# The shift of both LayerNorms moves from VectorE to GpSimd, in a cross-attention and expert kernel

## The reference

```
h  = layernorm(x)                        # over the 1024 positions, eps 1e-5
q, k, v = Wq h + bq, Wk ctx + bk, Wv ctx + bv      # 128x128 weights over the channels
att = softmax over a window of 16 keys around each position, 8 heads of 16 channels
x  = x + Wo att(q, k, v) + bo
g  = layernorm(x)                        # second LayerNorm
w  = top-2 of softmax(g @ gate_w.T) over 8 experts, renormalised
x  = x + sum_e w[:, e] * (g @ A_e.T @ B_e.T)       # rank 64 per expert
layernorm(x) = (x - mean) / sqrt(var + eps)
```

## Time and profile before

| what | value |
|---|---|
| median of 3 runs | 1264.25 us (1264.19 to 1271.45) |
| profiled execution, its own time | 1263.59 us |
| span of its trace | 1261.8 us |
| mean granted TensorE clock | 0.916 |
| one step of the batch loop | 35 to 40 us |

### The profile page before, as it was taken

The page is one execution under the profiler, slowest core; times in us unless marked ns, Lnnn a source line. Parts: engine busy times, 40 slices in busy tenths (PEclk is TensorE's granted clock), DMA queues, the critical chain, the costliest instruction groups (busy, mean ns, idle before and its releaser), DMA issues.

```text
span 1261.8 us, 55007 instructions
## 1 busy us (share of the span) xinstructions
PE 1074.9 (85%) x24452; PEld 909.8 (72%) x24452; DVE 898.5 (71%) x1922; ACT 574.4 (46%) x809; POOL 416.9 (33%) x306
## 2 busy tenths in 40 slices
PE   4658898988989888998988989888988888989986
PEld 2547786776778677776776878677876777877875
DVE  3567777776768767777776778777677776778873
ACT  4545535444545444444444444444454444455431
POOL 3563323333323233233333223233233333323220
PEclk8778998889989889988989989989988989989999
DMA  4422233123232123232123232123231232332210
GB/s 169 121 70 53 70 87 80 47 67 87 70 86 72 51 70 86 71 86 66 57 70 87 70 87 66 59 67 87 71 86 42 64 86 71 87 86 69 55 36 34
DMA packets 157313, 92.87 MB, mean 74 GB/s; under 512 B 139680, under 2 KB 139808, under 8 KB 156704
## 3 DMA queue, kind: packets, MB, share of 16 engines
q1 hardware_dynamic: 157088, 89.25, 25.4%
HBM read 55.16 MB, written 16.78 MB: 57 GB/s over the span
## 4 chain that ended last, share of the span: by engine, by line
issue 43%; POOL 20%; PE 16%; DVE 13%; ACT 4%; DMA 2%; SPq 1%; POOLq 0%; DVEq 0%
PE bank_a L310 8%; POOL prob L911 8%; POOL ctx_split L917 5%; PE bank_c L310 3%; POOL x_split L943 3%; PE bank_b L360 3%; POOL attn_split L934 2%; DVE row_max L744 2%; DVE row_sum L758 1%; PE bank_b L339 1%; DMA raw<-x 1%; ACT k_sb L575 1%; DVE prob L750 1%; SPq L246 1%; DVE stats L673 1%
## 5 line engine op out<-in xcount | busy, mean ns | idle before, releaser
L911 POOL TENSOR_TENSOR prob<-prob,row_inv 128x512 f32<-128x512 f32 x128 | 134.4, 1050 | 427.8 <-DVE row_inv L762 426.1
L360 PEld LDWEIGHTS bank_b<-prob_t,v_diag 64*64 64x64 f32 x4608 | 214.3, 148 | 49.2 <-issue 26.2
L360 PE MATMUL bank_b<-prob_t,v_diag 64*64 64x96 f32 (+2 forms) x4608 | 228.8, 257 | 15.4 <-DMA v_diag<-v_t 14.4
L310 PE MATMUL bank_a<-down_split,mid_split 128*128 128x264 f32 (+1 forms) x1536 | 215.9, 289 | 8.5 <-issue 6.8
L310 PEld LDWEIGHTS bank_a<-down_split,mid_split 128*128 128x128 f32 x1536 | 194.8, 189 | 16.5 <-issue 8.6
L769 DVE STREAM_TRANSPOSE prob_t<-prob 128x768 f32<-128x768 f32 x128 | 124.9, 976 | 111.8 <-POOL prob L911 110.6
L310 PE MATMUL bank_a<-up_split,ht_split 128*128 128x512 f32 x768 | 194.3, 402 | 3.5 <-DVE ht_split L859 3.5
L558 ACT ACTIVATE prob<-prob 128x512 f32<-128x512 f32 x128 | 80.8, 631 | 248.5 <-DVE prob L750 248.3
L339 PEld LDWEIGHTS bank_b<-k_sb,q_diag 32*32 32x32 f32 x16384 | 153.4, 104 | 39.5 <-issue 33.3
L339 PE MATMUL bank_b<-k_sb,q_diag 32*32 32x32 f32 x16384 | 169.1, 194 | 9.3 <-issue 6.5
L310 PEld LDWEIGHTS bank_a<-up_split,ht_split 128*128 128x128 f32 x768 | 141.0, 190 | 34.1 <-ACT ht_split L634 3.4
(11 more groups left out here) (76 smaller groups left out, 1360.6 us busy)
## 6 DMA issues: line engine op xcount, KB each, us to landing
v_diag<-v_t SPq DMA_DIRECT2D x128, 132.0 KB
raw<-x SPq DMA_DIRECT2D x32, 512.0 KB, 4.1
resid_pair<-x SPq DMA_DIRECT2D x32, 512.0 KB, 4.4
out<-resid_pair SPq DMA_DIRECT2D x32, 512.0 KB, 2.6
raw<-ctx SPq DMA_DIRECT2D x31, 512.0 KB, 3.6
prob_t<-up_w SPq DMA_DIRECT2D x1, 1024.0 KB, 6.3
resid_pair<-up_w SPq DMA_DIRECT2D x1, 1024.0 KB, 5.7
v_diag<-down_w SPq DMA_DIRECT2D x1, 1024.0 KB, 7.6
```

Source lines behind the costliest of these rows:

```text
L310: return nc.tensor.matmul(dst, st[:, s, st_cols], mv[:, m, mv_cols], start=start and n == 0, stop=stop and n == 2)
L360: last = nc.tensor.matmul(bank_b[2 + m % 2][rows, lo * PW:hi * PW], value_blocks(b)[rows, n, :], prob_t[rows, at:at + (hi - lo) * KT], sta ...
L911: nc.gpsimd.tensor_tensor(weights_of(m), weights_of(m), row_inv[:, cols].unsqueeze(2).broadcast_to([P, CT, KT]), ALU.mult).then_inc(prob_d ...
```

## The change

VectorE no longer computes the shift. Instead it computes the negated mean right behind `var_eps` (a `tensor_scalar` of one element), and GpSimd multiplies it with `rstd` right behind its power, after a wait on its own power. ScalarE waits for the new semaphores `shift1` and `shift2`. `var_eps` gets a second column per norm. No order of any engine is changed otherwise.

```
-        var_eps = sb("var_eps", [P, 2])
+        var_eps = sb("var_eps", [P, 2, 2])
...
+        shift1, shift2 = sem("shift1"), sem("shift2")
...
                 if later:
-                    act.wait_ge(ln1_step, later.count(6, 6))
+                    act.wait_ge(shift1, later.count(1, 1))
...
                 if prev:
-                    act.wait_ge(ln2_step, prev.count(6, 6))
+                    act.wait_ge(shift2, prev.count(1, 1))
...
-                nc.vector.tensor_scalar(var_eps[:, which:which + 1], moments[:, which, 1:2], EPS, None,
+                nc.vector.tensor_scalar(var_eps[:, which, 0:1], moments[:, which, 1:2], EPS, None,
                                         ALU.add).then_inc(semaphore, 1)
-
-            def layernorm_shift(which, semaphore, batch):
-
-                nc.vector.scalar_tensor_tensor(shift[:, which:which + 1], moments[:, which, 0:1], -1.0,
-                                               rstd[:, which:which + 1], ALU.mult,
-                                               ALU.mult).then_inc(semaphore, 1)
+                nc.vector.tensor_scalar(var_eps[:, which, 1:2], moments[:, which, 0:1], -1.0, None,
+                                        ALU.mult).then_inc(semaphore, 1)
...
                 if later:
                     first_norm()
-                    first_shift()
...
-                if prev and not cur:
-                    second_shift()
...
                     join_heads(cur, 1)
-                    if prev:
-                        second_shift()
...
+            def rows_norm(which, step_done, ready, b):
+
+                pool.wait_ge(step_done, b.count(6, 6))
+                nc.gpsimd.tensor_tensor(rstd[:, which:which + 1], var_eps[:, which, 0:1], consts[:, 2:3],
+                                        ALU.pow).then_inc(ready[0], 1)
+                pool.wait_ge(ready[0], b.count(1, 1))
+                nc.gpsimd.tensor_tensor(shift[:, which:which + 1], var_eps[:, which, 1:2],
+                                        rstd[:, which:which + 1], ALU.mult).then_inc(ready[1], 1)
...
                 if later:
-                    pool.wait_ge(ln1_step, later.count(6, 5))
-                    nc.gpsimd.tensor_tensor(rstd[:, 0:1], var_eps[:, 0:1], consts[:, 2:3],
-                                            ALU.pow).then_inc(rstd1, 1)
+                    rows_norm(0, ln1_step, (rstd1, shift1), later)
...
                     if prev:
-                        pool.wait_ge(ln2_step, prev.count(6, 5))
-                        nc.gpsimd.tensor_tensor(rstd[:, 1:2], var_eps[:, 1:2], consts[:, 2:3],
-                                                ALU.pow).then_inc(rstd2, 1)
+                        rows_norm(1, ln2_step, (rstd2, shift2), prev)
```

More of the change, by code:

```diff
@@ L802, in second_norm @@
                     layernorm_stats(1, resid[prev.parity], ln2_step, prev)
-                def second_shift():
-                    dve.wait_ge(rstd2, prev.count(1, 1))
-                    layernorm_shift(1, ln2_step, prev)
                 def first_norm():
@@ L812, in first_norm @@
                     layernorm_stats(0, raw, ln1_step, later)
-                def first_shift():
-                    dve.wait_ge(rstd1, later.count(1, 1))
-                    layernorm_shift(0, ln1_step, later)
                 if cur:
```

## The result

The changed kernel took 1287.47 us (median of 4 runs, 1285.57 to 1296.89), the kernel before 1266.51 us beside it (4 runs): ratio 1.0177, 95% interval 1.0129 to 1.0225. So the change costs some 21 us. The profiled execution of the changed kernel is its slowest one, 1296.89 us with a span of 1295.1, so its span is some 9 us longer than that of the median run; the reading goes by single steps.

The account below looks back on a forecast made before the run. It took a slackless loop through `h_sb` to bound the kernel, TensorE being nearly the bound. With `h_sb` 0.70 us later in 28 steps, +19.6 us on 1263.59 gives 1283 us; range 1250 to 1292.

Parts of the forecast that it names:

- The loop and its leverage: Batch loop: no slack, so a shift of `h_sb` by D moves each step by D while TensorE still waits; 28 steps.
- GpSimd's chain: GpSimd, first norm: own wait 0.06 us, multiplication 0.20; shift ready at 606.45, `attn_split` starts at 606.42 and its delay is hidden.
- L709 passes with a margin of 0.02: Gate chain on VectorE: L709 at 606.23 falls between the power's end and the multiplication at 606.25, so is not held.
- the first rival: Gate chain: L709 or the cast meets the multiplication and is held to `attn_split`'s end; 1250 us, or 1260; chance 0.17.
- its mixtures: Some steps as forecast, others with L709 too late; half and half 1266 us, other mixtures 1255 to 1278; chance 0.12.
- L716 is held to the end of `attn_split`: Gate chain on VectorE: two-input L716, due at 607.04, is held to 608.81, giving back the 2.32 us and 0.33 more.
- `x_split` is ready early and holds the rest: GpSimd: `x_split` starts at 608.96 instead of 611.88, runs 2.35 us to 611.31 and holds the gate chain's last steps.
- Which step it holds: Under `x_split`: L719's second half is held, `h_sb` 0.70 us later; if only L723 is held, 0.44.
- by turns: Rival: steps fall either way between forecast and L709 arriving too late; +3 us at half and half, 1266; chance 0.12.
- The mis-sized term: Per step, `h_sb` starts 0.70 us later (bounds 0.39 to 1.22), in 28 steps: +19.6 us.
- No price for the clock: TensorE: no further clock loss priced, as it runs at 0.50 behind these waits already; a longer wait might stretch that.
- The second norm at nothing: Second norm: xn starts some 0.2 us later, covered by ScalarE's 1.07 us idle; costs nothing, else 0.2 us a step.

Follow-up runs that it names:

- e1: Changed kernel, with GpSimd waiting for the gate chain's end before `x_split`; 1198.85 us, ratio 0.9446 against the kernel before.
- e5: Kernel before, plus GpSimd's added wait and a multiplication into an unused tile, the shift staying on VectorE; 1246.66 us, ratio 0.985.
- e4: Kernel before, with VectorE's shift as a `tensor_scalar` taking `rstd` as scalar operand instead of a second tensor input; 1233.54 us, ratio 0.9732.
- e6: Changed kernel, with `attn_split` ahead of the power and first-norm shift in GpSimd's order, no further wait; 1132.1 us, ratio 0.8907.

## Why the prediction was right

It said 1283 us, 28 x 0.70 = 19.6 us above the profiled execution; measured were 21 us between the medians, and 1287.47. By its own steps:

- *The loop and its leverage* (each step moves by what `h_sb` moves): 28 x (6.42 - 5.62) = 22 us against 21 between the medians. In the other direction it understates: e1, e5 and e4 gained 68, 22 and 34 us where 28 steps give 39, 14 and 22. Between the profiled executions, path and fall of TensorE's busy time add up well there (58, 22 and 28 us for spans shorter by 61, 22 and 28). So that the path alone gives the change's 21 us is in part luck, as the clock below shows.
- *GpSimd's chain*: wait and multiplication about as costed. The wait took 0.08 us for 0.06 and the shift 0.19 for 0.20, and `attn_split` started 1.06 us behind `var_eps` where the prediction had 1.08.
- *L709 passes with a margin of 0.02*: as L706 it started 0.03 to 0.04 us ahead of the multiplication in all 28 steps. Its longest in the whole trace is 0.153 us, so the first rival came in none of the steps. The range of 1250 to 1266 that I kept for it and for its mixtures was not needed. The cast did not fall between power and multiplication, by the prediction's own figures either: it starts 0.04 us before the power ends (606.15 against 606.19; measured 580.52 against 580.56). It was not held, and the further powers show that a power holds nothing, so "held while GpSimd runs a `TENSOR_TENSOR`" was too wide.
- *L716 is held to the end of `attn_split`*: 583.21 against 583.19, with a start 1.69 behind `var_eps`, predicted 1.70. It is L713 in the changed kernel.
- *`x_split` is ready early and holds the rest*: started 3.62 behind `var_eps`, predicted 3.62.
- *Which step it holds*: a pick, as taken by the nearest row, the cast, and not the sum, which kept 0.17 us. It is the second pick, as worked out, in 17 steps; in 11 it is the first, which the prediction had starting 0.12 us ahead of `x_split` and passing. This went by turns, not L709. The rule of the Trainium skill ("VectorE: DVE Perf Modes", section "Mode 2×_2P") fits the trace: eight elements from one input are held (2.66 us for the two picks), one element is not; that they ran in that mode no run here shows. The other rule of the Trainium skill ("SBUF — State Buffer", section "Who interferes with whom"), that whoever issues first has the port, fits e5 and both kernels with further powers, but not by the starts in the trace when they are close: a pick that started 0.09 us before `x_split` was the one held.
- *The mis-sized term* is that 0.70: measured 0.80 in the step shown and 0.79 in the mean of all 28. In the step shown the first pick was held, and the second had its own 0.28 us still to run: it ended at 585.91, 0.22 us after `x_split`, and not 0.02. `h_sb` then came 0.20 us behind the sum's start in place of the 0.29 of the earlier trace rows, which takes 0.09 of it back.
- *No price for the clock*: the prediction had TensorE at 0.50 behind these waits already. In the earlier trace rows that holds for the output projection, but the transposes ahead of it ran at full clock. In the step shown TensorE waited 3.57 us and not 1.65, and ran the transposes at half its clock too (0.50, 1.2 GHz): 1.11 us, and 0.66 in the earlier trace rows. The stretches below (length, busy time of PE, PEld, DVE, ACT and POOL, PEclk, DMA) show it, first the kernel before, then the changed one. Transposes of `h_sb` and output projection each took 3.4 us more over the span, and TensorE's busy time rose from 1074.9 to 1091.5 us in all. The spans of these two executions are 33 us apart, 22 of them the path's; the medians are 21 apart, which leaves the clock nothing. What it cost the median run is not settled.

```profile
613.00:615.00 2.00, 0.66 (x4) 0.42 (x4) 1.28 (x4) 2.00 (x4) 1.78 (x2) 1.00 0.00 0
```

```profile
586.00:588.00 2.00, 0.00 (x0) 0.00 (x0) 1.93 (x5) 0.08 (x1) 0.00 (x0) 0.92 0.55 133
588.00:590.00 2.00, 1.11 (x4) 0.71 (x4) 1.47 (x4) 2.00 (x4) 0.36 (x1) 0.50 0.32 129
```

- *The second norm at nothing*: its cover was not taken away by any experiment, so that this is free was only argued.

## What to carry to other kernels

Before moving a small operation off an engine, look what the long instructions of GpSimd hold: a one-element instruction of 2.3 us that ends with a GpSimd instruction is a queue at a port, not work, and taking it away can let the next one that needs the port queue there. Then ask when each long GpSimd instruction starts relative to the short chain; moving it into idle time ahead of the chain was worth some 155 us to the changed kernel, and the form with a scalar operand in place of a second tensor 34 us to the kernel before. A change that looks bad can be good behind such a queue, so try it again once the queue is gone.

## What was unexpected in the hardware

- The order of arrival decides within hundredths of a us, but not simply by whose start comes first. Picks that started 0.090 to 0.096 us ahead of `x_split` were held to its end, those with 0.101 us or more passed; the same kernel measured again was as sharp (held up to 0.100, passed from 0.102). A pick takes 0.29 us, so what passed was over 0.19 us after `x_split`'s start: an estimate of when it takes the port.
- One-element work on GpSimd held nothing. e5's 32 shifts of the first norm started 0.04 us ahead of the multiplication and took 0.16 us, and gate products inside a power took 0.16.
- GpSimd lets a waiting VectorE instruction in between two long ones that stand back to back (the second pick of the kernel with two further powers).
- 0.55 us more of useless work on GpSimd made the kernel 123 us faster (1300.66 to 1177.29).
- A VectorE instruction with one input of one element and a scalar operand is not held (0.21 us at 0.07 us into `attn_split`); one with one input of eight elements can be (a single pick, up to 2.48 us).
- Gains came out larger than the path gives (68 for 39 us in e1, 134 for 81 in e6), and TensorE's busy time fell along with them (by 21 and 58 us) at a higher mean granted clock (0.940 and 0.971 for 0.916); the loss came out at the path's value between the medians.
